# A four-layer graph network on one core: a tile's own nodes leave the gathered neighbour lists

## The reference

```
_w  = (1.0 + jnp.arange(4096)) ** (-0.5);  _w = _w / _w.mean()
_a  = uniform(4096, 4096) < clip(0.000976562 * _w[:, None] * _w[None, :], 0, 1)
_a  = logical_or(_a, eye(4096));  adj = _a * uniform(4096, 4096, 0.05, 1)

h = relu(layernorm(x)); x = x + ((adj @ h + beta*h) / (sum(adj, 1) + beta)) @ k0 + b0
h = relu(layernorm(x)); x = x + softmax(where(adj != 0, adj * (h @ Hv), -1e30)) @ h
h = relu(layernorm(x)); x = x + relu(concat(h, adj @ h) @ W.T + b)
h = relu(layernorm(x)); x = x + transformer_conv(h, adj)   # 4 heads of 32, softmax over the neighbours, gated skip
```

## Time and profile before

| | us |
|---|---|
| median of 3 runs (lowest, highest) | 1194.56 (1192.62, 1199.07) |
| the profiled execution | 1195.47 |
| its span, first to last instruction | 1193.8 |
| PE busy | 895.6 (75%) |
| DVE busy | 835.5 (70%) |
| ACT busy | 681.3 (57%) |
| POOL busy | 656.0 (55%) |
| mean granted TensorE clock | 0.843 |

### The profile page before, as it was taken

How to read it: one execution, slowest core, us unless ns; L and a number is a source line. 1 busy time by engine, 2 the same in 40 slices (tenths; PEclk the granted TensorE clock), 3 DMA queues, 4 the chain that set the end, 5 groups by cost and what they waited for, 6 DMA issues and landing times.

```text
span 1193.8 us, 24673 instructions
## 1 busy us (share of the span) xinstructions
PE 895.6 (75%) x5760; PEld 565.9 (47%) x5760; DVE 835.5 (70%) x2260; ACT 681.3 (57%) x3070; POOL 656.0 (55%) x662
## 2 busy tenths in 40 slices
PE   4979999999999541677667639998685888878860
PEld 1535455454554320565556525554453555555540
DVE  7378889889898774666666673121555888888888
ACT  4999887977979040344343433000364787878862
POOL 4003778764464636777777700777516666666640
PEclk9988998999989665566675569999796999999995
DMA  9656767566471217444445446993324444444421
GB/s 370 203 203 239 254 218 284 210 215 250 175 260 42 62 43 227 131 124 132 126 127 136 125 163 263 394 328 114 95 102 123 125 124 127 124 118 121 121 76 71
DMA packets 89668, 201.26 MB, mean 169 GB/s; under 512 B 20576, under 2 KB 61920, under 8 KB 83808
## 3 DMA queue, kind: packets, MB, share of 16 engines
q10 hardware_dynamic: 9216, 83.38, 18.1%
q1 hardware_dynamic: 58592, 66.35, 16.9%
q0 software_dynamic: 21760, 50.46, 15.3%
HBM read 168.27 MB, written 28.98 MB: 165 GB/s over the span
## 4 chain that ended last, share of the span: by engine, by line
DVE 29%; PE 26%; issue 16%; POOL 10%; DMA 8%; DVEq 3%; ACT 2%; POOLq 0%; ACTq 0%; SPq 0%
POOL work L749 9%; PE ps L1827 7%; DVE work L1216 5%; DMA work<-kv_table,node_flat 3%; DVE work L1217 3%; PE ps L1802 2%; PE ps L1871 2%; DVE work L1527 2%; DMA work<-h_table,node_flat 2%; PE ps L1880 2%; PE ps L1672 2%; DVE work L1145 2%; PE ps L1668 2%; DVE work L1140 1%; PE ps L1818 1%
## 5 line engine op out<-in xcount | busy, mean ns | idle before, releaser
L888 ACT ACTIVATE unread<-work 128x128 bf16<-128x128 f32 x1024 | 300.7, 295 | 5.1
L1719 PE MATMUL ps<-work,h_wide 128*128 128x512 f32 x512 | 242.6, 630 | 17.9 <-ACT h_wide L800 17.9
L705 POOL DMA_INDIRECT work<-in_adj_rows,adj_stage x152 | 203.9, 1342 | 66.9 <-issue 35.3
L888 ACT ACTIVATION_READ_ACCUMULATOR unread<-work 128x1 f32 x1024 | 191.1, 187 | 0.0
L749 POOL DMA_INDIRECT work<-h_table,stage x140 | 133.0, 950 | 97.3 <-DMA h_table<-h_wide 55.0
L1719 PEld LDWEIGHTS ps<-work,h_wide 128*128 128x128 f32 x512 | 102.1, 205 | 141.2 <-issue 139.4
L749 POOL DMA_INDIRECT work<-kv_table,node_flat x124 | 118.5, 955 | 89.9 <-PE ps L1890 33.4
L749 POOL DMA_INDIRECT work<-h_table,node_flat x124 | 118.0, 952 | 45.1 <-issue 37.9
L1527 DVE CUSTOM_DVE_ANT_0 work<-ps,work 128x512 f32<-128x512 f32 x168 | 116.0, 746 | 18.1 <-PE ps L1871 18.0
L981 ACT ACTIVATE work<-work 128x512 f32<-128x512 f32 x165 | 117.0, 714 | 0.9 <-DVE work L1536 0.8
L1880 PE MATMUL ps<-ident,work 128*128 128x128 f32 x648 | 93.3, 281 | 31.9 <-ACT work L981 23.0
(11 more groups left out here) (225 smaller groups left out, 1678.1 us busy)
## 6 DMA issues: line engine op xcount, KB each, us to landing
work<-in_adj_rows ACTq DMA_DIRECT2D x38, 2048.0 KB, 7.9
work<-adj_table SPq DMA_DIRECT2D x66, 256.0 KB, 4.7
work<-in_adj_rows SPq DMA_DIRECT2D x6, 2048.0 KB, 11.8
adj_table<-work SPq DMA_DIRECT2D x80, 128.0 KB, 1.9
mask_table<-work SPq DMA_DIRECT2D x43, 128.0 KB, 1.8
work<-mask_table SPq DMA_DIRECT2D x43, 128.0 KB
kv_table<-work SPq DMA_DIRECT2D x32, 128.0 KB, 1.7
work<-work SPq DMA_DIRECT2D x43, 64.0 KB
```

The lines of the kernel that those rows point to most:

```text
L705: nc.gpsimd.indirect_dma_start(out=ag[:, h, c, :], out_offset=None, in_=adj_rows, in_offset=bass.IndirectOffsetOnAxis(ap=adj_stage[:, h // ...
L888: ins = nc.scalar.activation(unread[:, m % (MQ // 2) * TB + t, :], ring[:, q, m, t * P:(t + 1) * P], ACT.Abs, accum_out=seen[:, b, t, q * ...
L1719: ins = mm(ps[:, 0, :], h_sb[:, q * MQ + m, :], ring[:, q, m, :], start=(q + m == 0), stop=False)
```

## The change

The nodes of a tile are no longer in its own list. A group is now three gathered chunks (`GC` = 3, 384 entries) and a fourth chunk that is always the tile's own 128 nodes. SP loads that fourth chunk: its node rows with a plain strided DMA from the node table, and its adjacency from 32 further blocks of `adj_rows`, which are laid out on the host. Only the first group of a tile gets its real own adjacency; further groups of the same tile read a block of zeros. Two small tables (`quad_own`, `quad_row`) tell SP which block and which tile it is. Everything behind the gathers still works on four chunks.

```diff
+GC = QC - 1
+GW = GC * P
+PARTS = (HALF, GC - HALF)
+NP = -(-N // GW)
...
             def mark(nb):
...
-                nc.vector.tensor_scalar(flag[:, :, :], seen_of(nb)[:, :, :], 0.0, None, ALU.not_equal).then_inc(flag_ready, 1)
+                nc.vector.scalar_tensor_tensor(flag[:, :, :], seen_of(nb)[:, :, :], 0.0, other[:, :, bass.ds(T - TB * nb, T)],
+                                               ALU.not_equal, ALU.mult).then_inc(flag_ready, 1)
...
+                    nc.vector.tensor_scalar(quad_row[:, :], quad_tile[:, :], T - 1, None, ALU.min)
...
+                    nc.vector.scalar_tensor_tensor(quad_own[:, :], quad_row[:, :], 1.0, quad_first[:, :], ALU.add, ALU.mult)
...
             def gather_half(i, h):
...
-                for c in range(HALF):
+                for c in range(PARTS[h % 2]):
...
                 def load(g):
...
-                    sp.dma_start(ac[:, b, :, :], adj_table[bass.ds(q * P + P, P), :]
-                                 .rearrange("p (c n) -> p c n", c=QC)).then_inc(ac_full[k][b], 16)
+                    sp.dma_start(ac[:, b, 0:GC, :], adj_table[bass.ds(q * P + P, P), :]
+                                 .rearrange("p (c n) -> p c n", c=GC)).then_inc(ac_full[k][b], 16)
+                    block = quad_value(sp, quad_own, q, T)
+                    sp.dma_start(ac[:, b, GC, :], adj_rows[bass.ds(block * P + ZERO_ROW, P), :]).then_inc(ac_full[k][b], 16)
+
+                def load_own(g):
+                    rows, table = tables_of(k)
+                    t = quad_value(sp, quad_row, g.q + begin, T - 1)
+                    own = table[0:N, :].rearrange("(p m) f -> p m f", p=P)[:, bass.ds(t, 1), :]
+                    sp.dma_start(rows[:, g.b, GC, :], own.rearrange("p m f -> p (m f)")).then_inc(
+                        ac_full[k][g.b] if k == 2 else own_full[g.b], 16)
...
                     if k == 1:
                         store_mask(g)
+                    sp.wait_ge(pv_done[k], g.q + 2)
+                    settle(sp)
+                    load_own(ahead)
+                    if k == 1:
                         mask_stored(g)
                 for b in range(bufs - 1):
                     load(Quad(0, b, bufs))
+                for b in range(TB):
+                    sp.wait_ge(row_stored[b], rows_of_before(k + 1))
+                for b in range(bufs - 1):
+                    load_own(Quad(0, b, bufs))
...
                 def gather(g):
...
-                    for c in range(QC):
-                        at = node_flat[:, QC * g.q + c:QC * g.q + c + 1] if plain else stage[:, b, c:c + 1]
+                    for c in range(GC):
+                        at = node_flat[:, GC * g.q + c:GC * g.q + c + 1] if plain else stage[:, b, c:c + 1]
...
+    own = [tiles[t, :, t // TB, t % TB, :] for t in range(T)]
+    blocks = np.concatenate([blocks, np.zeros((P, P), blocks.dtype)] + own)
```

More of the change, by code:

```diff
@@ L124, in build @@
         gate = sb("gate", [P, TB, T])
+        other = sb("other", [P, TB, 2 * T])
         iota_j = sb("iota_j", [P, TB, NP])
@@ L253, in build @@
         ac_full[3], hg_full[3] = ac_full[1], hg_full[1]
+        own_full = [sem(f"own_full_{b}") for b in range(NBUF)]
         link_a = sem("link_a")
@@ L608, in load_adj @@
                     adj_loaded(sp, k, Quad(steps, b, bufs), steps)
+                    settle(sp)
+                    own_loaded(sp, k, Quad(steps, b, bufs), steps)
                     settle(sp)
@@ L667, in _ @@
             nc.gpsimd.memset(gate[:, :, :], 1.0).then_inc(iotas, 1)
-            pool.wait_ge(iotas, 12)
+            nc.gpsimd.memset(other[:, :, :], 1.0).then_inc(iotas, 1)
+            pool.wait_ge(iotas, 13)
+            nc.gpsimd.affine_select(out=other[:, :, :], in_=other[:, :, :], compare_op=ALU.not_equal, fill=0.0,
+                                    base=-T, pattern=[[-1, TB], [1, 2 * T]], channel_multiplier=0).then_inc(iotas, 1)
             nc.gpsimd.memset(gate[:, :, 0:1], 0.0).then_inc(iotas, 1)
@@ L687, in _ @@
                 spare = (QUADS + BEHIND + 1 + h // 2) * P
-                for n in range(2):
-                    pool.dma_start(adj_table[spare:spare + P, n * HALF * P:(n + 1) * HALF * P]
-                                   .rearrange("p (c n) -> p c n", c=HALF), ag[:, h, :, :]).then_inc(ag_full[h], 16)
+                chunks, columns = part(h)
+                pool.dma_start(adj_table[spare:spare + P, columns]
+                               .rearrange("p (c n) -> p c n", n=P), ag[:, h, chunks, :]).then_inc(ag_full[h], 16)
             def place_quad(i, n):
@@ L1437, in step2 @@
                 settle(dve)
-                nc.vector.tensor_copy(stage[:, b, :], node_flat[:, bass.ds(QC * (ahead.q + begin2), QC)]).then_inc(staged2, 1)
+                nc.vector.tensor_copy(stage[:, b, :], node_flat[:, bass.ds(GC * (ahead.q + begin2), GC)]).then_inc(staged2, 1)
                 dve.wait_ge(pv_done[2], q + 3)
@@ L1632, in _ @@
                 tiles = slice(FT * i, FT * i + FT)
[L1633 removed]
+                nc.vector.tensor_tensor(x_sb[:, tiles, :], x_sb[:, tiles, :], xr[:, tiles, :], ALU.add).then_inc(link_e[3], 1)
             further = further_turns(dve)
@@ L1928 @@
     blocks = tiles.transpose(2, 1, 0, 3, 4).reshape(ZERO_ROW, P)
-    blocks = np.concatenate([blocks, np.zeros((P, P), blocks.dtype)])
+    own = [tiles[t, :, t // TB, t % TB, :] for t in range(T)]
+    blocks = np.concatenate([blocks, np.zeros((P, P), blocks.dtype)] + own)
     arrays = {
```

99 lines of the change are left out of this document (52 added, 47 removed).

## The result

The changed kernel takes 1150.24 us (median of 4 runs, 1148.34 to 1152.18) where the kernel before takes 1193.59 (4 runs beside it). The ratio is 0.963, with a 95% interval of 0.959 to 0.967. The profiled execution took 1148.34 us, with a span of 1146.6 and a mean granted clock of 0.883. The forecast was 1148.

The account below looks back on a forecast made before the run. POOL's gather issue bounds layer two, PE layer three's dense part, DVE layer four. Terms +1 - 0.5 - 31.6 - 12.8 - 2 - 1 = -46.9 take 1195.47 to 1148.6; the median, 0.9 lower, gives 1148 us, range 1130 to 1172.

Parts of the forecast that it names:

- Layer two, -31.6: Layer two: three POOL gathers a group instead of four shorten the 39 steps from 199.0 to 167.4 us.
- Between 3.9 and 4.47 I take 4.2: Layer two: step time in us, between DVE's limit at full clock and the PE and ACT path at low clock.
- I add 0.3 us a step: Layer two, last 12 steps: allowance for POOL waiting on SP's later loads, 3.6 us in all.
- the first rival: Layer two: SP becomes the limit, 5.0 us a step comes back, total 1180 us; chance 0.14.
- 2.6 is well under 4.2: Layer two: SP's four DMAs and two register loads, 2.6 us a step, fit within the 4.2 us step.
- POOL should wait for PE's value product in most steps: Layer two: sign expected in the new trace if the forecast held.
- The spacing: Layer two: value products 4.0 to 4.5 us apart in the new trace; staying at 5 would refute the prediction.
- the clock: Layer two: granted clock above 0.7, from 0.61, because PE would be busy for over 85% of a step.
- Layer three, -12.8: End of layer three: earlier last gather starts layer four's projection at 835 instead of 847.8; idle stretch 19 to 6 us.
- Between the layers: Before layer two: first logits gain 0.5 us; with 1 us added by the first layer's larger `mark`, net +0.5.
- The start of layer four: Layer four's start: fewer gathers before the first and third groups of keys gain 2 us.
- its rounds: Layer four's steady part: DVE stays the limit at 5.85 us a round; fewer PE waits for gathers gain 1 us.

Follow-up runs that it names:

- four-gather runs: Changed kernel, but in layer two POOL gathers a fourth chunk and SP loads no own rows; 1263.4 us and 1271.6 us on two slower chips.

## Why the prediction was right, and where it was not

**Layer two, -31.6, measured -30.5.** The step was right in kind: POOL's issue was the limit, and one gather in four off its queue is the gain. The Trainium skill (page "DMA: Bandwidth & Descriptors", section "Issuing engines are not separate DMA queues") says that a second issuing engine saves the issuer's time to start a DMA and no more, and that this is usually small beside the DMA. The saving is of that kind here, but it isn't small: 1.25 us of POOL's queue a gather, beside 3.8 us from issue to landing, and where the queue is the limit it is the step. The four-gather runs, where the rule would have nothing change, took 0.9 to 1.0 us more a step, on chips where standstills are part of it. The size was right by two errors that cancel, 2.2 us too long in the first 28 steps and 3.5 too short in the last. "Between 3.9 and 4.47 I take 4.2" stood for a limit by PE and ACT; the first 28 steps took 4.12, in quiet stretches 3.80, with POOL and DVE in balance. DVE's limit at full clock, put at 3.9, was measured at 3.81. "I add 0.3 us a step" for the last 12 was too little: they took 0.65 more than 4.2 us, where SP has hardly any slack. That is the first rival, in those steps alone. What was offered as its refutation, "2.6 is well under 4.2" (3.3 with the list), left out the waits' own instructions and the gaps between DMAs, which add up one behind another; in the trace SP's stream is 4.4 to 4.6 us a step almost without a wait for another engine.

**What would show it.** "POOL should wait for PE's value product in most steps" was wrong: 12 of 40. The spacing (4.12, then 4.85; mean 4.33) and the clock (0.77) were as said. But the argument for the clock, by PE's busy share, was not: that share fell from 66% to 61% in layer two while the clock rose. Windows of 20 us in the changed kernel's layer two, a quiet one and one late:

```profile
500.00:520.00 20.00, 11.45 (x81) 9.31 (x82) 16.52 (x58) 10.79 (x26) 15.14 (x16) 1.00 0.59 170
600.00:620.00 20.00, 13.51 (x66) 11.37 (x65) 13.56 (x47) 8.83 (x22) 12.12 (x13) 0.67 0.52 140
```

The full level is granted in a stretch in which PE is busy for 57%, and a mix of the two levels in one with 68%. Why the clock rose is not shown.

**Layer three, -12.8, measured -9.5.** The gathers did come early enough, and PE's stretch behind the dense part fell from 19.1 to 9.6 us, not to 6. The term assumed that one matmul group and one addition stand behind the last landing. In fact four groups remain behind the dense part, and from one of DVE's additions to the next it is 1.6 to 1.7 us, unseen before because they waited for POOL's rows. Removing the late gather laid this bare.

**Starts.** Between the layers the sum had +0.5 with the first layer and got -1.4: DVE's larger `mark` did not lengthen the path, and the own rows did gate the logits, as said and as the runs with own rows first bear out. The start of layer four (-1.9 for -2) and its rounds (-2.0 for -1) were right: DVE bounds them, and own rows are not late; two, three or four gathers give 236.5, 236.6 and 238.6.

**The total** came out as near as it did partly by luck: layer two and the end of layer three gave 4.4 us less than forecast, and rows that had been put at nothing or at less gave that back.

**On the slower chips** the change gains 10%, not 4%. Nothing in the trace of before hinted at that.

## What to carry to other kernels

Where an engine's queue of indirect DMAs is the limit, count what each one holds it for (here 1.25 us) and give the ones with a regular pattern to another queue, where a plain one costs 0.35 us and its register value some 0.6; it pays until the next engine's own stream is as long, so add that stream up with its gaps before the second step. Price the queue that takes over by the distance of its instructions end to end, register values included, and in the steps where it has most to do; here a sum of 2.6 to 3.3 us was 4.4 to 4.6 in the trace. When a late transfer is removed, ask who stood idle behind it and what that engine's own pace is.

## What the runs showed of the hardware that was not expected

- Chips can differ much on one program: the kernel before took 1194 and 1198 us in two sets of runs and 1363 to 1379 on two other chips (14 to 15% more), the changed kernel 1150 on the first and 1226 on one of those, with the same busy times of single instructions (a gather 0.94 to 0.95 us, ACT's copy 0.60).
- On the two slower ones several engines stand still together, ACT's copy for up to 5.7 us in the changed kernel and 11.4 with four gathers; where this was followed, it lay in rows of back-to-back gathers on POOL. The fewer of these a kernel has, the nearer the chips come: 169 to 185 us apart with 588 gathers, 76 with 447.
- The granted clock was 1.00 in a stretch where PE was busy for 57% and 0.67 in one with 68%.
